# First stage of a two-layer kernel: the expert gates go through DRAM and multiply x_n on GpSimd, in place of TensorE and VectorE

## What is computed

```python
y   = attention_in_windows(norm(x))            # Q, K, V, output: 1x1 convolutions
x1  = x + y
x_n = norm(x1)                                 # over the 64 channels
p   = softmax(x_n @ router_w + router_b)       # 8 experts
top_p, top_i = top_k(p, 2); top_p /= sum(top_p)
x2  = x1 + sum_e gate_e * (x_n @ expert_w[e] + expert_b[e])   # gate_e is 0 off the top two
```

## Time and profile before

| | us |
|---|---|
| median of 3 runs | 8791.29 (8777.52 to 8808.5) |
| the profiled execution, its own time | 8805.53 |
| its span, first to last instruction | 8803.7 |
| PE busy, DVE busy | 6314.4, 6682.1 |
| ACT busy, POOL busy | 4408.5, 5536.3 |

### The profile page before, as it was taken

The page is one execution under the profiler, slowest core; times in us unless marked ns, Lnnn a source line. Parts: engine busy times, 40 slices in busy tenths (PEclk is TensorE's granted clock), DMA queues, the critical chain, the costliest instruction groups (busy, mean ns, idle before and its releaser), DMA issues. The chain is left out here.

```text
span 8803.7 us, 102835 instructions
## 1 busy us (share of the span) xinstructions
PE 6314.4 (72%) x30290; PEld 2534.8 (29%) x30290; DVE 6682.1 (76%) x7810; ACT 4408.5 (50%) x5988; POOL 5536.3 (63%) x2731
## 2 busy tenths in 40 slices
PE   5888888888885767667777766677776766776555
PEld 3444444444442222222222222222222222222133
DVE  3555555555555999999999999999999999999634
ACT  1222222222223766666666666666666667676400
POOL 0000000000004999999999999999999999999600
PEclk8887787787877888887788888887788888788666
DMA  1111111111113555555555555555556555555553
GB/s 30 42 38 42 36 42 38 38 43 36 38 40 115 193 195 198 187 207 185 208 183 205 186 201 194 195 199 192 201 183 210 183 204 186 203 191 197 152 151 128
DMA packets 513971, 1253.45 MB, mean 142 GB/s; under 512 B 170085, under 2 KB 172297, under 8 KB 513673
## 3 DMA queue, kind: packets, MB, share of 16 engines
q1 hardware_dynamic: 513417, 1252.41, 42.2%
q0 software_dynamic: 512, 0.53, 0.0%
HBM read 943.30 MB, written 231.21 MB: 133 GB/s over the span
## 5 line engine op out<-in xcount | busy, mean ns | idle before, releaser
L1177 DVE TENSOR_TENSOR_SCAN b_h<-b_a,b_h 128x448 f32<-128x448 f32 x3584 | 3677.3, 1074 | 294.0 <-POOL b_h L1002 148.2
L1014 POOL TENSOR_TENSOR b_h<-b_h,b_ct 128x896 f32<-128x896 f32 x1792 | 3692.1, 2090 | 24.2 <-DVE b_h L1177 16.6
L1105 ACT ACTIVATE b_a<-b_dts,decay 128x441 f32<-128x441 f32 x3584 | 2227.4, 629 | 1583.9 <-DVE b_h L1177 1564.3
L1264 PE MATMUL b_b<-b_rows,spread_b 16*128 16x512 f32 (+1 forms) x1792 | 697.9, 786 | 1487.5 <-DVE b_h L1167 1486.5
L1025 POOL MEMSET b_seq<- 128x938 f32 x2 | 1.7, 882 | 2645.9 <-POOLq L789 2645.9
L1167 DVE TENSOR_TENSOR b_h<-b_dus,b_b 128x896 f32<-128x896 f32 x1344 | 1432.9, 1066 | 73.7 <-DMA b_dus<-d_dtu 71.3
L490 DVE TENSOR_TENSOR a_xg<-a_xd,a_pb 128x784 f32<-128x784 f32 x512 | 495.3, 967 | 637.7 <-PE a_pb L604 635.5
L1272 PE MATMUL b_y<-b_h,fold 128*32 128x512 f32 (+1 forms) x7168 | 953.7, 659 | 6.8 <-POOL b_h L1014 6.8
L1002 POOL TENSOR_TENSOR b_h<-b_dus,b_bt 128x896 f32<-128x896 f32 x448 | 936.5, 2091 | 10.5 <-DMA b_dus<-d_dtu 10.5
L1264 PEld LDWEIGHTS b_b<-b_rows,spread_b 16*128 16x128 f32 x1792 | 167.4, 228 | 1756.4 <-DVE b_h L1167 1754.7
L1233 PE MATMUL b_w<-b_seq,w_conv 128*128 128x384 f32 (+1 forms) x896 | 540.5, 765 | 12.5 <-DMA b_seq<-b_seq 12.5
(11 more groups left out here) (208 smaller groups left out, 8940.3 us busy)
## 6 DMA issues: line engine op xcount, KB each, us to landing
b_bt<-d_rows SPq DMA_DIRECT2D x448, 448.0 KB, 6.0
b_ct<-d_rows SPq DMA_DIRECT2D x448, 448.0 KB, 3.6
b_dts<-d_dt SPq DMA_DIRECT2D x448, 448.0 KB, 6.0
b_dus<-d_dtu SPq DMA_DIRECT2D x448, 448.0 KB, 6.0
a_xd<-a_xn SPq DMA_DIRECT2D x256, 196.0 KB, 3.4
d_dt<-b_dt SPq DMA_DIRECT2D x112, 448.0 KB, 2.6
d_dtu<-b_soft SPq DMA_DIRECT2D x112, 448.0 KB, 2.5
b_seq<-b_seq SPq DMA_DIRECT2D x112, 234.0 KB, 3.5
```

What stands on the lines that cost most here:

```text
L1014: nc.gpsimd.tensor_tensor(hh[t][:], hh[t][:], ct[t // 4 % 2][:], ALU.mult).then_inc(hc_done, 1)
L1105: a(steps(bank(aa, k)), steps(half(dts[t % 4], k)), ACT.Exp, scale=decay[:, t % 4, t // 4:t // 4 + 1]).then_inc(a_done, 1)
L1177: v.tensor_tensor_scan(half(hh[t], k), bank(aa, k), half(hh[t], k), 0.0, ALU.mult, ALU.add).then_inc(h_done, 1)
L1264: last = mm(bb[:, lo:hi], spread_b[q, row, :], rows[i][q, lo:hi], start=True, stop=True)
```

## The change

- The split in three bf16 parts goes (four instructions on DVE), and with it `ident_bf`, `pick`, `b_exp3` and their setup. The multiplication L537 that ends the gates now stands ahead of the two `xw` instructions.
- PE turns the float32 gates themselves, seven matmuls into 16 rows, and does it ahead of the query-key product. ACT's copy to `gt` (now 16 rows, float32) stands ahead of its copy of that product.
- SP stores `gt` to a new DRAM buffer `gates_d`, waits for that and for the end of the other slot's experts, and then issues eight loads, one for each expert. Each reads two rows of 784 float32 (one per image) and writes each of them to 64 partitions of `xg[x]`. The eight `xg` buffers are shared by both slots.
- POOL multiplies `xd` onto each `xg[x]` in place. `spread_gate` on PE and L490 on DVE are gone.
- PE runs the experts in four pairs at fixed places: after the scores, after the turned probabilities, after the output, and after the last average. The bias is a float32 product with 16 rows in place of three bf16 ones with 48.
- The setup has four DMAs fewer, and fewer small instructions.

```diff
+gt = sb("a_gt", [2 * NE, TA])
+gates_d = nc.dram_tensor("d_gates", [SLOTS, 2 * NE, TA], F32, kind="Internal").ap()
-xg = [sbuf(f"a_xg{i}", [P, TA], F32, st) for i in range(4 * SLOTS)]
+xg = [sbuf(f"a_xg{i}", [P, TA], F32, st) for i in range(NE)]
 ...
 # SP
+def gates(m, im):
+    own_no, other_no = 16 * im + 16, im + m
+    sp.wait_ge(gt_ready[m], im + 1)
+    sp.dma_start(gates_d[m], gt[m][:]).then_inc(gates_stored[m], 16)
+    sp.wait_ge(acc_ready[1 - m], other_no)
+    sp.wait_ge(gates_stored[m], own_no)
+    for x in range(NE):
+        r0 = NE * (x % 2) + 2 * (x // 2)
+        src = gates_d[m, r0:r0 + 2, :].unsqueeze(1).broadcast_to([2, C, TA])
+        sp.dma_start(xg[x][:], src).then_inc(gate_in[x], 16)
 for k in range(NP):
     with sp.Fori(0 if k else 2, HALF) as j:
         it = j + (k * HALF + 1)
+        gates(1, it - 2)
         load(0, k, j, it)
         copies(0, it - 1)
         store(1, it - 2)
+        gates(0, it - 1)
         load(1, k, j, it)
         copies(1, it - 1)
         store(0, it - 1)
 # POOL
+def half(s, it, m, im):
+    pool.wait_ge(copied[m], 64 * im + 32)
+    for x in range(NE):
+        pool.wait_ge(gate_in[x], 32 * im + 16 * m)
+        nc.gpsimd.tensor_tensor(xg[x][:], xd[2 * m + x % 2][:], xg[x][:], ALU.mult).then_inc(xg_ready[m], 1)
 # DVE
-v.tensor_tensor(xg[4 * m + x % 4][:], xd[2 * m + x % 2][:], pb[m][:, 0:TA], ALU.mult).then_inc(xg_ready[m], 1)
 # PE
-def spread_gate(x):
-    for a, b in banks(TA):
-        last = mm(pb[m][:, a:b], pick[:, NE // 2 * (x % 2) + x // 2, :], gt[m][:, a:b], start=True, stop=True)
+def experts(pair):
+    pe.wait_ge(xg_ready[m], NE * im + 2 * pair + 2)
+    for a, b in banks(TA):
+        for i in range(2):
+            mm(pa[m][C * i:C * i + C, a:b], w_exp[:, pair, :], xg[2 * pair + i][:, a:b], start=(pair == 0), stop=False)
...
```

More of the change, by code:

```diff
@@ L174, in program @@
                 ]
-                for part in range(3):
-                    r0 = 16 * part + NE * i
-                    loads.append((b_exp[r0:r0 + NE, c0:c0 + C], expert_b))
+                loads.append((b_exp[NE * i:NE * i + NE, c0:c0 + C], expert_b))
             for n, v in enumerate((gamma, beta, mean, var)):
@@ L392, in _ @@
                         copies(0, 1)
+                        gates(0, 1)
                         load(1, 0, 1, 2)
@@ L528, in half @@
                                 v.reciprocal(g1[m][:], g1[m][:]).then_inc(small[m], 1)
+                                chain(16)
+                                v.tensor_tensor(o1[m][:], o1[m][:], wide, ALU.mult).then_inc(small[m], 1)
                             if s is not None:
@@ L625, in half @@
                                 strip(pb[s], average[:], sq[s]).then_inc(var_ready[s], 1)
+                            if m is not None:
+                                pe.wait_ge(small[m], SMALL * im + SMALL)
+                                for r in range(WIN):
+                                    last = mm(pb[m][0:2 * NE, r * P:r * P + W], o1[m][:, 2 * r:2 * r + 2, :].rearrange("p i e -> p (i e)"),
+                                              ident[0:W, 0:W], start=True, stop=True)
+                                last.then_inc(gtr_ready[m], 1)
+                            if s is not None:
                                 pe.wait_ge(xw_ready[s], 2 * it + 2)
@@ L630, in half @@
                                 last.then_inc(t_ready[s], 1)
-                            if m is not None:
-                                pe.wait_ge(small[m], SMALL * im + SMALL)
-                                for r in range(WIN):
-                                    last = mm(pb[m][0:48, r * P:r * P + W], g3[m][:, r, :], ident_bf[0:W, 0:W],
-                                              start=True, stop=True)
-                                last.then_inc(gtr_ready[m], 1)
-                                pe.wait_ge(gt_ready[m], im + 1)
-                                spread_gate(0)
-                            if s is not None:
                                 pe.wait_ge(pads_zero, 2 * SLOTS)
@@ L688, in half @@
                             if m is not None:
-                                experts(7, 8)
-                                for n in range(3):
-                                    for a, b in banks(TA):
-                                        last = mm(pa[m][:, a:b], b_exp3[:, n, :], gt[m][:, a:b], start=False, stop=(n == 2))
+                                pe.wait_ge(gt_ready[m], im + 1)
+                                experts(3)
+                                for a, b in banks(TA):
+                                    last = mm(pa[m][:, a:b], b_exp[:], gt[m][:, a:b], start=False, stop=True)
                                 last.then_inc(acc_ready[m], 1)
```

105 lines of the change are left out of this document (22 added, 83 removed).

## The result

The changed kernel takes 11,834.42 us (median; 11,832.07 to 11,851.27), the kernel before 8784.41 beside it: 1.347 times as long, with a 95% interval of 1.344 to 1.351. The prediction was 11,675, with a range of 11,250 to 12,700.

The account below looks back on a forecast made before the run. No engine is full; stage A's half is a chain of 40.8 us, which two-engine loads stretch to 85.7. 63 intervals give +2829, the last half +57, setup less 3: +2883, so 11,675 us, range 11,250 to 12,700.

Parts of the forecast that it names:

- Two engines for a load: Gate loads in stage A: two source rows outside give two DMA engines of 16, so 7.9 us a load, 63.2 for eight.
- The 25.4 GB/s of one engine: Speed of one DMA engine in the gate loads, from 419 GB/s at share 1.03, not the x load's 20.3.
- rival 2: Gate loads on two engines at or beyond the slower 20.3 GB/s each: half 101.6 us, time 12,700; chance 0.08.
- Up to the first product: From L495's start through small chain, turning, copy, store and first load to POOL's first product: 20.5 us.
- The small chain: DVE's small instructions on the gates from L495's start, with L537 added: 5.2 us.
- Between first and last product: POOL's eight products, each waiting for its load, with loads 7.9 us each: 55.3 us.
- From the last product to L493: End of the half: POOL's last product, then PE's last pair 2.88, bias 2.98 and router; 9.9 us.
- The handovers: Seven handovers between engines along the half's chain, some 0.07 us each, taking 85.2 to 85.7.
- The setup: Before stage A: four issues of 0.34 us and some small instructions saved, 3 us at most.
- SP's queue: x loads, copies and store wait behind gates in SP's in-order queue; costed at nothing.
- Rival 1: Gate loads use all 16 engines, POOL sets the pace: half about 37.8 us, time 8610; chance 0.08.
- Rival 3: 16 engines, but the gates' round trip through DRAM eats the gain: half 40.8 us, 8790 to 8900; chance 0.03.

Follow-up runs that it names:

- Experiment 2: The changed kernel with each load reading 4, 8 or 16 gate rows in place of two (wrong gates): ratios 1.090, 1.006 and 0.978 to the kernel before.
- experiment 1: The changed kernel with each load issued as two DMAs of one row to 64 partitions: 8608.68 us, ratio 0.979 to the kernel before.
- experiment 4: The kernel before with only the changed order: gates finished, split, turned and copied earlier, no DRAM or GpSimd: 8646.88 us, ratio 0.984.

## Why the prediction was right

**Two engines for a load.** This step decided the sign and the size, and it held: 50 GB/s, a share of 2/16, loads 7.98 us apart (7.9 predicted). Experiment 2 shows that the count follows the source's outer rows even where the destination has 128: shares of 0.13, 0.26, 0.52 and 1.02 of 16 engines with 2, 4, 8 and 16 rows. These four agree with the rule of the Trainium skill (page "DMA: Bandwidth & Descriptors", section "Why a DMA increments its semaphore by 16 and not by 1").

**The 25.4 GB/s of one engine** held for two engines at 25. It was right not to take the x load's 20.3; rival 2 would have given 9.9 us a load.

**Up to the first product: 20.5 us predicted, 22.4 measured.** The small chain was right (5.2). PE came to the turning at 6.6, since it did the average before it at the lower clock, and took 1.98 where 1.55 was taken: 8.6 for 6.8. The store of 49 KB let the first load be issued 1.75 us later, not 2.5. The first load then took 11.3 us to the product, not 10.4.

**Between first and last product: 55.3 us predicted, 55.9 measured.** The loads stood 7.98 apart for 7.9.

**From the last product to L493: 9.9 predicted, 10.4 measured.** Pair and bias took 2.88 and 2.98, as said. The router's product to the next start is the term that I mis-sized: 2.83, since it too ran at the lower clock, where 1.59 was taken. The handovers, and the pair and bias with them, were taken about 0.7 too large.

So 88.8 for 85.7 in this half and 88.0 in the mean. Times 63 the mean's difference is 2.3 x 63, some 144 us, nearly all of the 159 that the forecast of 11,675 is short of. In this half one mistake in two places makes 1.8 and 1.2 us of the 3.1: I took the lower clock for the pair and the bias, behind a wait, and not for the router's product right behind them, nor for the average and the turning that follow. The other errors are as large, 0.9 (first load) and 0.6 (between the products) too small, 0.75 (store) and 0.7 (handovers) too large. They cancel, and that is luck. In the mean the router's product is busy for 2.5 us and the turning for 1.8, against 2.8 and 2.0 here, so the mean half is shorter than the one shown.

**The setup** was to save up to 3 us; the first gates came 0.6 us later than before. Over all kernels of this case they start between 93.1 and 98.9, so this says nothing for or against the saving.

**SP's queue** was costed at nothing, and it cost nothing, but not for the reason in full. SP was held for 47 us by the issues themselves, and the x load was issued only at 1566.65. It is needed a half later, so nothing waited. The `copies` came at 1582.84, ahead of the last load's end and not after the loads, as the prediction had it. That cost nothing that shows: the last two products stand 8.2 us apart, as do the two before.

**Rival 1** is what experiment 1 built. It named 8610 us and 37.8 a half; 8609 and 37.6 were measured. The hit is in part luck, since its working was less good. A load on all engines took not 1.0 us but 401,408 B / 250 GB/s = 1.6, hidden by GpSimd's 1.9. It took the 3 us from the removed spread gates and an earlier first pair, as the ping-pong of the earlier trace rows suggested; the order alone gives 2.7 us with the ping-pong in place (experiment 4). And the last half, of which it says nothing, took 36.6 us in place of 28.1. Its limit of about 8 engines held: with 8 rows outside the ratio was 1.006. **Rival 3**, the DRAM trip that eats the gain, did not come.

## What to carry to other kernels

Count the rows in the slowest dimension of both sides of a DMA before you cost it: a broadcast of two rows to 128 partitions ran on two engines of sixteen, and the same bytes in two DMAs of 64 rows removed 3226 us. When a change loses, undo its smallest suspicious detail first, since the rest may be a gain that the detail hides. And where an edit moves work as well as replacing it, run the move alone: here it gave 2.7 of the 3.2 us that experiment 1 gained in a half, and no gate had to go through DRAM for it.

## What was not expected of the hardware

**A queue is held by its own issues.** An issue on SP took 0.3 to 0.6 us in most rows, but the eight loads of two rows held SP's queue for 47.17 us (0.5 to 12.4 each, some at the same time, 7.0 in the median), and the next load behind them took 7.57. With 4 rows outside the eight took 20.2 us, with 8 5.6 to 6.0, with 16 5.3, and the sixteen of experiment 1 10.1. Why is not shown.

**The form of a 16-engine load sets its rate**: 236 to 250 GB/s for 16 by 8 and for the halves of 64 partitions, 375 for the plain 128 rows. The Trainium skill (page "SBUF — State Buffer", section "Door 1: The DMA port swizzle") says that the rate depends on how many of 16 ports the partitions written reach, and that partitions 0 to 63 reach half of them. The halves of experiment 1 agree with this in sign. The 16 by 8 loads reach all 128 partitions, as the plain ones do, and ran at 236 all the same, so this rule as it stands doesn't account for them; which partitions are written at one moment no row shows.

**DVE and GpSimd slow each other.** In before DVE's product of two operands in SBUF (`a_p` by `a_mx`) took 977 ns. Beside GpSimd's products it took 1987 in the mean in experiment 1 (1767 to 2357 in one window), and 976 again with the products on DVE. GpSimd's product went from 1835 to 1936 ns, 0.8 us more for the eight of a half. Products with an operand in PSUM stayed at 975. The Trainium skill (page "SBUF — State Buffer", section "SBUF: two separate sides") states a lock between the two engines for a VectorE instruction with both inputs in SBUF, beside a GpSimd one that reads SBUF; whoever starts first keeps it for the whole instruction. The numbers agree: the longest such product in experiment 1 took 2.37 us, less than a whole GpSimd product and its own 0.98 together, and the products with one input in PSUM were not slowed.
